# A gated cross-attention block with a routed feed-forward on one Trainium2 core: nine whole expert tiles are moved ahead of the ranking of the last batches

## The reference

```python
x = x + tanh(g_xattn[0]) * xattn(layernorm(x), ctx, mask)      # softmax(x ctx^T / sqrt(512)) ctx
x = x + tanh(g_ffn[0]) * ffn(layernorm(x), w_router, w_gate, w_up, w_down)
# ffn: probs = softmax(xt @ w_router.T); top_v, top_i = top_k(probs, 2); top_v /= sum(top_v)
#      g, u = xt @ w_gate, xt @ w_up (192 wide per expert); act = silu(g) * u
#      out = sum over the two experts of comb * (act @ w_down)
```

## Time and profile before

| what | value |
|---|---|
| three runs | 295.83, 294.32, 295.79 us, median 295.79 |
| the profiled execution | 297.36 us, of it the span from first to last instruction 295.5 us |
| busy: PE, VectorE, ACT, POOL | 88%, 58%, 50%, 55% of the span |
| granted TensorE clock, mean | 0.929 |
| moved by DMA | 52.08 MB, mean 176 GB/s |

### The profile page before, as it was taken

The page is one execution under the profiler, slowest core; times in us unless marked ns, Lnnn a source line. Parts: engine busy times, 40 slices in busy tenths (PEclk is TensorE's granted clock), DMA queues, the critical chain, the costliest instruction groups (busy, mean ns, idle before and its releaser), DMA issues.

```text
span 295.5 us, 5447 instructions
## 1 busy us (share of the span) xinstructions
PE 259.2 (88%) x1501; PEld 220.4 (75%) x1501; DVE 172.2 (58%) x650; ACT 147.3 (50%) x310; POOL 163.9 (55%) x151
## 2 busy tenths in 40 slices
PE   0899998995999978546999999999999999999940
PEld 0777775683867747436899999999999999999930
DVE  4577779996786888992244444344444444444420
ACT  3469856773568544221155555444455444544430
POOL 1256656453455446515236787784884848747461
PEclk9999999999699997556799999999999999999995
DMA  6996888776899634503436588576795886958583
GB/s 207 379 380 197 293 289 293 262 272 222 261 304 328 213 109 152 171 3 87 132 56 114 118 141 148 83 146 133 129 164 100 169 159 104 175 95 159 119 131 50
DMA packets 25950, 52.08 MB, mean 176 GB/s; under 512 B 5248, under 2 KB 5376, under 8 KB 25920
## 3 DMA queue, kind: packets, MB, share of 16 engines
q0 software_dynamic: 8304, 19.83, 36.9%
q1 hardware_dynamic: 17616, 31.89, 32.2%
HBM read 33.81 MB, written 17.89 MB: 175 GB/s over the span
## 4 chain that ended last, share of the span: by engine, by line
PE 63%; DVE 13%; DMA 11%; issue 4%; ACT 3%; SPq 3%; POOL 1%; POOLq 0%; ACTq 0%; DVEq 0%
PE S L1068 9%; PE S L1072 9%; PE S L1069 9%; PE A L1058 6%; DMA out<-X 5%; PE S L930 5%; PE PO L941 4%; DMA x2s<-Y 2%; DVE TB L716 2%; DMA X<-in_x 2%; DVE st L604 2%; PE PL L1091 2%; PE PO L1091 1%; PE PO L1093 1%; PE PL L1095 1%
## 5 line engine op out<-in xcount | busy, mean ns | idle before, releaser
L441 POOL DMA_INDIRECT out<-YT,IXI x36 | 56.8, 1577 | 41.9 <-issue 19.7
L1068 PE MATMUL S<-WGh,XTh 128*128 x144 | 51.8, 360 | 1.0 <-ACT XTh L536 1.0
L1069 PE MATMUL S<-WGl,XTh 128*128 x144 | 48.9, 340 | 0.0
L415 POOL DMA_INDIRECT XG<-x2s,IXG x39 | 38.5, 987 | 18.0 <-issue 9.7
L870 DVE TENSOR_TENSOR H<-SG,S 128x192 f32<-128x192 f32 x36 | 12.7, 354 | 47.8 <-ACT SG L543 41.5
L385 POOL TENSOR_TENSOR WGl<-WGl,WGh 128x512 fp32r<-128x512 f32 x24 | 30.7, 1283 | 16.3 <-ACT WGh L500 16.3
L543 ACT ACTIVATE SG<-S 128x192 f32<-128x192 f32 x36 | 11.9, 330 | 50.1 <-PE S L1072 46.0
L376 POOL TENSOR_TENSOR rs<-mv,CS 128x1 f32<-128x1 f32 x32 | 17.7, 554 | 32.6 <-DVE mv L610 32.6
L863 DVE TENSOR_TENSOR XTl<-A,XTh 128x512 fp32r<-128x512 f32 x37 | 25.6, 691 | 13.6 <-ACT XTh L536 13.1
L941 PE MATMUL PO<-CX,PT 128*128 128x512 f32 x64 | 31.2, 609 | 1.3 <-DVE X L650 1.3
L930 PE MATMUL S<-CT,XLT 128*128 128x256 f32 x128 | 31.7, 392 | 0.0
(11 more groups left out here) (153 smaller groups left out, 548.0 us busy)
## 6 DMA issues: line engine op xcount, KB each, us to landing
WGl<-in_wgu SPq DMA_DIRECT2D x24, 256.0 KB, 4.6
X<-in_x SPq DMA_DIRECT2D x16, 256.0 KB, 4.0
CT<-in_ctxt SPq DMA_DIRECT2D x8, 512.0 KB, 5.8
CX<-in_ctxn SPq DMA_DIRECT2D x8, 512.0 KB, 5.5
out<-X SPq DMA_DIRECT2D x16, 256.0 KB, 4.7
x2s<-Y SPq DMA_DIRECT2D x16, 256.0 KB, 4.8
WD1l<-in_wd SPq DMA_DIRECT2D x8, 256.0 KB, 4.5
WS<-in_wd SPq DMA_DIRECT2D x8, 256.0 KB, 4.5
```

Of the source, the lines that this page charges most:

```text
L415: pool.indirect_dma_start(out=XG[:, j % NX, :], out_offset=None, in_=x2s, in_offset=bass.IndirectOffsetOnAxis(ap=IXG[:, j:j + 1], axis=0))\
L441: pool.indirect_dma_start(out=out, out_offset=bass.IndirectOffsetOnAxis(ap=IXI[:, j:j + 1], axis=0), in_=YT[:, j % NB, :], in_offset=None, ...
L1068: pe.matmul(o, XTh[:, j % 2, c, :], WGh[:, bass.ds(e, 1), c, :], start=(c == 0), stop=False)
L1069: pe.matmul(o, XTh[:, j % 2, c, :], WGl[:, bass.ds(e, 1), c, :], start=False, stop=False)
```

## The change

Nine tiles (`NE`) of the first `EB` = 4 batches are listed, gathered and run while the last batches are still ranked. A tile is whole when its expert has a further 128 rows after four batches. By the counts above twelve are whole (2, 1, 1, 1, 2, 2, 2, 1); the first nine are of the experts 0, 0, 1, 2, 3, 4, 4, 5, 5. The other 27 live tiles follow, again from expert 0: 2, 3, 4, 4, 3, 3, 4, 4 tiles. At tile 9 POOL waits for all earlier adds whatever the expert.

All 40 weight units are split in attention, up to three in a step, and the tile loop holds none. The expert buffers (XG, XTh, XTl, SG, H, HTh, HTl, YT) lie over those of attention (X, CT, CX, XL, XLT, P, PT) so that each gather waits only for the stores of the X tiles under its buffer; ranking's own buffers are outside that overlay. Since ranking goes on during the first tiles, the tile loop uses one bank for transposes (A0), one for the down product (PO), and the bank of gate and up (S0, S1) also for the activation's transposes. On PE, VectorE, ACT and POOL the ends of attention and ranking stand between the parts of tiles 0 to 8, by an order written out by hand (`SIDES` gives VectorE's side steps after mul, coef and hlo of each tile). Two of the exponentials for the router's weights are made on POOL (`odds`), so that ACT keeps the table for Silu.

```diff
-SPLIT = [0, 1, 1] + [2] * 15 + [1] * 4
-NUA = NU - 4
-HOLD = [3, 5, 7, 9]
+SPLIT = [0, 1, 1, 3, 2, 3, 3, 2, 3, 3, 2, 3, 3, 3, 2, 3, 3]
+EB = 4
+NE = 4 * EB - 7
+NEP = (NE + 3) // 4 * 4
+NL = 32
+SIDES = [(2, 2, 5), (2, 2, 3), (1, 1, 2), (1, 1, 2), (2, 2, 2), (2, 2, 3), (1, 3, 4), (2, 1, 2)] + [(0, 0, 0)] * 31
...
             def loadw(u):
+                if u >= NST:
+                    sp.wait_ge(s_wh, u - NST + 1)
...
+            def odds(b):
+                pool.wait_ge(s_dd, b + 1)
+                pool.wait_ge(s_cb, b)
+                pool.tensor_tensor(out=e2[:, :, 0], in0=euler.to_broadcast([128, 2]), in1=dd[:, :, 0], op=ALU.pow)\
+                    .then_inc(s_e2, 1)
+            def stored(*tiles):
+                pool.wait_ge(s_y2, max(tiles) + 1)
+                for k in tiles:
+                    pool.wait_ge(s_so[k % NXT], 16 * (k // NXT + 1))
...
+            for s in range(NTK + 3):
+                for u in units(s - 1)[0:1]:
+                    lo(u)
+                if 0 <= s - 3 < NTK:
+                    rstd(mv2, s - 3, rs2, s_st2, s_rs2)
+                if s == NTK + 2:
+                    odds(6)
+                    stored(13)
+                    gather(3)
+                for u in units(s - 1)[1:]:
+                    lo(u)
+                if s + 2 < NTK:
+                    rstd(mv1, s + 2, rs1, s_st1, s_rs1)
+                if s == NTK:
+                    pool.wait_ge(s_ixe, 1)
+                    pool.wait_ge(s_sy[0], 16 * EB)
+                    pool.wait_ge(s_sy[1], 16 * EB)
+                    pool.wait_ge(s_scb[0], 16 * EB)
+                    stored(9, 10)
+                    gather(0)
+                    stored(11)
+                    gather(1)
+                if s == NTK + 1:
+                    stored(12)
+                    gather(2)
...
+            stored(14, 15)
+            for j in range(4, NX):
                 gather(j)
...
             for j in range(NT):
                 with lives(pool, live, j):
+                    if j == 1:
+                        odds(7)
                     pool.wait_ge(s_y, j + 1)
-                    if j:
+                    if j == NE:
+                        landed(j)
+                    elif j:
                         fence(j)
...
+                    if j + NX == NE:
+                        pool.wait_ge(s_ixg, 1)
+                        pool.wait_ge(s_sy[0], 16 * 8)
+                        pool.wait_ge(s_sy[1], 16 * 8)
+                        pool.wait_ge(s_scb[1], 16 * (B - EB))
                     if j + NX < NT:
                         gather(j + NX)
-                    if j in HOLD:
-                        lo(NUA + HOLD.index(j))
...
+            side += [coefs(5), top2(6), taken()]
+            weave(queue(x2(14), first_xlo(), nbias(mv2, rs2, nb2, 14, s_rs2, s_nb2), x2(15)), 2)
+            side += [slots(5), ranks(6), coefs(6),
+                     braid(slots(6), queue(top2(7), braid(ranks(7), coefs(7)))),
+                     braid(slots(7), left()), last_tiles()]
             live = None
             for j in range(NT):
                 with lives(dve, live, j):
                     mul(j)
+                    if j == 0:
+                        for _ in nbias(mv2, rs2, nb2, 15, s_rs2, s_nb2):
+                            pass
...
+                    steps(SIDES[j][0])
                     if j + 1 < NT:
                         xlo(j + 1)
...
                     coef(j)
+                    steps(SIDES[j][1])
                     hlo(j)
+                    steps(SIDES[j][2])
...
+            tp(14)
+            score(15)
+            first_list()
+            pv(14)
+            rt(12)
+            t2(13)
+            tp(15)
...
+            pe.wait_ge(s_ixe, 1)
...
             tx(0)
+            pv(15)
+            rt(13)
+            own, live = experts(0, ERE, 0), None
+            pe.wait_ge(s_wl, NU)
             for j in range(NT):
                 with lives(pe, live, j):
                     gu(j, own[j])
+                    if j == 0:
+                        t2(14)
+                    if j == 1:
+                        t2(15)
+                        rt(14)
                     if j + 1 < NT:
                         tx(j + 1)
+                    if j == 0:
+                        cum(5)
+                    if j == 2:
+                        tab(5)
+                        cum(6)
+                    if j == 4:
+                        cum(7)
+                        count()
+                    if j == 5:
+                        tab(6)
+                    if j == 6:
+                        last_list()
+                        tab(7)
...
                     if j >= 1:
                         down(j - 1, own[j - 1])
+                    if j == 1:
+                        rt(15)
+                    if j == 6:
+                        last_rows()
                     th(j)
+                    if j == 0:
+                        tab(4)
```

More of the change, by code:

```diff
@@ L266, in units @@
         def units(s):
-            return range(*[min(NUA, sum(SPLIT[:max(0, n)])) for n in (s, s + 1)])
+            return range(*[min(NU, sum(SPLIT[:max(0, n)])) for n in (s, s + 1)])
         STEPS = NTK + 9
@@ L333, in _ @@
                     loadw(u)
-                if s == NTK + 3:
-                    for u in range(NUA, NU):
-                        loadw(u)
                 k = s - 4
@@ L414, in gather @@
                     pool.wait_ge(s_cj, j - NX + 1)
-                pool.indirect_dma_start(out=XG[:, j % NX, :], out_offset=None, in_=x2s,
-                                        in_offset=bass.IndirectOffsetOnAxis(ap=IXG[:, j:j + 1], axis=0))\
+                rows, at = (x2s[0:EB * S, :], IXE[:, j:j + 1]) if j < NE else (x2s, IXG[:, j - NE:j - NE + 1])
+                pool.indirect_dma_start(out=XG[:, xg(j), :], out_offset=None, in_=rows,
+                                        in_offset=bass.IndirectOffsetOnAxis(ap=at, axis=0))\
                     .then_inc(s_g[j % NX], 16)
@@ L428, in fence @@
                     landed(j)
-            for j in range(NX):
+            rstd(mv1, 0, rs1, s_st1, s_rs1)
+            rstd(mv1, 1, rs1, s_st1, s_rs1)
+            for s in range(NTK + 3):
[23 more added lines that the diff above has]
+                    gather(2)
@@ L556, in yev @@
                     act.wait_ge(s_add[j % NB], 16 * (j // NB))
-                act.activation(YT[:, j % NB, :], (PO, PL)[j % 2][:, :], ACT.Copy, scale=cj[:, j % 4:j % 4 + 1])\
+                act.activation(YT[:, j % NB, :], PO[:, :], ACT.Copy, scale=cj[:, j % 4:j % 4 + 1])\
                     .then_inc(s_y, 1)
+            xln(0)
+            for s in range(NTK + 1):
+                if 0 <= s - 4 < NTK:
+                    ev2(s - 4)
+                if s < NTK:
+                    ev1(s)
+                if s + 1 < NTK:
+                    xln(s + 1)
+                if 0 <= s - 2 < NTK:
+                    evp(s - 2)
+                if s >= 7 and s % 2 == 1 and (s - 7) // 2 < B:
+                    weigh((s - 7) // 2)
+                if 0 <= s - 3 < NTK:
+                    x2ln(s - 3)
+                if 0 <= s - 1 < NTK:
+                    exp(s - 1)
+                for u in units(s):
+                    hi(u)
+            ev2(13)
+            evp(15)
+            weigh(5)
+            act.activation(rsum[:, 0:1], rinv[:, 0:1], ACT.Silu)
             xhi(0)
+            x2ln(14)
             live = None
@@ L658, in top2 @@
                 for i in range(2):
[L659 removed]
+                    n = mark(dve.max(out=mx[:, i, :], in_=PL[:, 8 * i:8 * i + 8]))
                     yield
```

567 lines of the change are left out of this document (323 added, 244 removed).

## The result

| | before | after |
|---|---|---|
| median of four runs each | 295.39 us (294.32 to 295.83) | 301.47 us (299.39 to 303.34) |
| ratio, 95% interval | | 1.019 (1.0129 to 1.025) |
| the profiled execution | 297.36 us, span 295.5 | 300.6 us, span 298.8 |
| busy: PE, VectorE, ACT, POOL | 88%, 58%, 50%, 55% | 86%, 59%, 49%, 55% |

A forecast was written before the change was run, and what follows sets the result against it. POOL's queue of scatters and fences was to set the end: IXG at 155.9 (102.3 + 4 + 13.6 + 23.5 + 4.5 + 1.9 + 6.1) plus 136.9 gives 292.8, 2.7 below 295.5; forecast 293.1 us, range 286 to 301.

The forecast's parts named there:

- The price of a fence step: POOL's tile queue: a step with a fence takes 6.3 us from scatter to scatter, a plain one 3.17.
- Rival 1: Tile loop: PE, not POOL, sets the end if a fence step costs under 5.3 us; 283.7 us, chance 0.15.
- Attention, +4: Up to score(15), 102.32 before: loading 40 weight units instead of 32 adds 4 us, ends -5 and +12.
- cost nothing of their own: Attention: eight more ACT copies and POOL subtractions (8 x 1.28) add no time, the engines being busy 36.6 and 28.9 of 56.3 us.
- From score(15) to the first tile, 13.6: After attention: PE waits for the 40th unit, done 13.6 us after score(15)'s start; first tile at 119.9 instead of 140.2.
- Tiles 0 to 5, 29.9: First six tiles: 23.5 us for tiles, 4.5 for PE work moved into them, 1.9 for a VectorE stall.
- the list 6.1 us into tile 6: Tile 6: the last index list, IXG, is ready 6.1 us after the tile's start, at 155.9.
- Rival 2: Attention: it stretches by +12 instead of +4, the index list comes later than 160 us, end 301; chance 0.22.
- POOL waits for IXG before gather(9): POOL's queue after scatter(3): POOL waits for the list IXG, near 155.9, with scatters 4, 5 and 6 queued behind.
- scatter(3) is through by about 153: POOL's early queue: scatter(1) from near 138.4, 2 and 3 behind fences of 6.3 each, scatter(3) done near 153.
- the one at 4 has long landed: POOL's queue after IXG: the fence before scatter(4) costs nothing, leaving ten fences to pay, 63.0 us.
- The queue from scatter(4) on: POOL after IXG and gather(9): ten fence steps 63.0 us, nineteen plain 60.2, the last two 4.4.

The follow-up runs named there:

- e6: Changed kernel, each tile's rows added into a DRAM tensor of its own, sum over experts left out, and no fences; 287.68 us, ratio 0.9706.
- e7: Kernel before with six further unconditional waits for all earlier adds, thirteen in all, nothing else; 309.53 us, ratio 1.0446.
- e3: Changed kernel, where the expert changes POOL issues gather(j+6) before the fence instead of after scatter(j); 290.12 us, ratio 0.9822.
- e8: Kernel before with only the new weight split, all 40 units in attention and none in the tile loop; 300.24 us, ratio 1.012.
- e11: Kernel before plus eight 256 KB DRAM-to-DRAM copies on SP's queue in attention, no added engine work; 300.78 us, ratio 1.02.
- e9: e8 with POOL's subtraction cut to 64 of 512 columns in gate, up and upper down units; 293.17 us, ratio 0.9955.
- e2: Changed kernel with another order of the weight units of experts 5 and 7 and SP's wait count adapted; 299.13 us, ratio 1.0108.
- e4: Changed kernel with the edits of e1, e2 and e3 together; 285.74 us, ratio 0.9636.
- e13: e8 with both reciprocal roots ahead of the second and third subtraction in each of POOL's steps; 298.82 us, ratio 1.0079.
- e10: Kernel before, its own 32-unit split, POOL's subtraction cut to 64 of 512 columns in gate, up and upper down units; 289.22 us, ratio 0.9863.
- e14: Changed kernel with POOL's subtraction cut to 64 of 512 columns in gate, up and upper down units; 297.33 us, ratio 1.0035.
- e1: Changed kernel with odds(7), the exponential of batch 7 on POOL, moved one tile later; 299.33 us, ratio 1.0099.

## Why the prediction was wrong

It had 293.1 us and -2.7; the time is 301.47, just outside the range of 286 to 301 and with the other sign. On the span the sum gave 292.8 and the trace has 298.8. The other 2.4 us of the 8.4 are the scale: the sum put the median 0.3 us above the span of before, while the median after lies 2.7 above its own.

**The bound was named rightly.** POOL's queue sets the end, by e6, e7 and e3. The price of a fence step, the term that the text called decisive, was 6.3. (Its 6.1 from the rows took off a subtraction that lies inside a fence's wait; the six steps of the kernel before, read one by one, average 6.3.) Between scatters 4 and 35 are 126.5 us where the sum had 127.6. With nineteen plain steps at 3.18 and two last ones at 1.9 the ten fences come out at 6.2 each. The 4.2 us estimated from the rule of the Trainium skill (DMA: Bandwidth & Descriptors, section Anatomy of one DMA) is not borne out for these indirect adds: 6.2 here. Rival 1 falls with it. One bank instead of two for transposes and the down product cost nothing that shows: with PE as the bound, in e6, the 21 steps from scatter(12) to scatter(33) take 3.92 us each, the period of the earlier trace rows.

**The terms that failed**, in order, with the time by which each moved the end:

1. *Attention, +4* was +7.4 (score(15) at 109.75), 3.4 more. It is the load of the weights: e8 has +7.8 from that part alone. The base of the term, 102.32, is one trace of an attention that ends at 99.31 in another; the stall of 66 to 77, which the prediction let vanish or come again, differs from trace to trace of the same code. The parts seen, each from its own run and not to be added: bytes and issues 2.1 to 5.1 us (e11, by copies that go another way), the short subtraction 3.7 (e9), the late buffer WS about 2 (e2, e4), the roots behind the second and third subtraction 1.4 at most (e13). The rest of the split is open. The reason given for "cost nothing of their own", a busy share of 28.9 of 56.3 us, is no reason: in the ranking of the kernel before the subtractions take 4.8 us (e10), with 40 units in attention 3.7 (e9). What the eight further ones cost by themselves no run separates.
2. *From score(15) to the first tile, 13.6* was 15.0, 1.4 more. The path was the one forecast, x2(14), rstd(14), two subtractions. x2(14) with its statistics ends at 121.02, 11.3 us after score(15) and not 10.3, and the 40th unit is done at 124.11. PE was not ready then: tx(0) had waited 2.66 us for the gather, pv(15) ran for 3.75 us where pv(14) took 1.96, and rt(13) behind it took 1.72 where 0.8 was forecast, which is the other 0.7. e14 gives 4.0 of this stretch back, at the full clock.
3. *Tiles 0 to 5, 29.9* were 29.0, and *the list 6.1 us into tile 6* was there after 4.95. So IXG came at 158.75, 2.9 us after the forecast, where the first tile was 4.9 late. Rival 2 put its bound at 160; it explains half of the miss.
4. *"POOL waits for IXG before gather(9)", "scatter(3) is through by about 153" and "the one at 4 has long landed".* Beside the size of point 1, this is the step that failed. `odds(7)` stands ahead of scatter(1) and waits for a side step of tile 3; the prediction listed POOL's scatters and gathers and left this instruction out. Scatter(3) came at 157.80, there was no wait for IXG, and scatter(4) paid its whole fence: 4.94 us from IXG to scatter(4), not 1.3. That is 3.6 us, by itself more than the forecast's gain. e1 gives the structure of the forecast back: scatter(3) at 153.26 and the wait for IXG.
5. *The queue from scatter(4) on* took 1.1 us less, *the tail* 8.6 us instead of 8.0.

Points 1 to 3 make the 2.9 of IXG. Together +2.9 + 3.6 - 1.1 + 0.6 = +6.0, the 298.8. Even with point 4 mended the change is not faster (e1, 1.0099): the gain of 2.7 was smaller than the 3.4 by which the attention term was off, inside its ends of -5 and +12, and 0.53 for faster was too much for a result that hung on it.

**What the gain of 13.5 us turned into:** six further expert changes on the queue that had no room left. The prediction saw that; it did not ask whether the 3 us idle in each fence could hold the gather, which turns the slower kernel into a faster one.

## What to carry to other kernels

When work is split in an early and a late group, count what is paid per change of group (here 7 expert changes became 13, at 3 us of pure waiting each), on the queue that pays for it. In a queue that waits for landings, put every issue that doesn't depend on the landing ahead of the wait. List *all* instructions of the bounding queue, the small ones with foreign waits above all, and don't cost POOL's elementwise work at nothing because its busy share is low: look at the longest duration of tiny VectorE instructions beside it, over all of them. And before a shift of a few us in one trace is given a cause, look at what the same code does in another.

## What the runs showed of the hardware

- A VectorE instruction of 128x16 elements takes 0.16 us at its shortest and 1.22 beside a POOL subtraction of 1.27. Another order on POOL moves the hold to other instructions: between e8 and e13 the four of MS fell from 5.0 to 0.6 us and those of cc rose from 0.6 to 3.8.
- pv(15) ran at 3.75 us, pv(14) at 1.96. Ahead of pv(15) PE had been idle for 2.66 and 0.66 us; the granted clock from 119.68 to 123.43 is 0.50, the lower of the two levels, 1.2 GHz. In e14 PE had been idle for 2.40 us, and pv(15) ran at 1.88 with a granted clock of 1.00.
- A second gather issued between an add and the wait for its landing does not lengthen the wait for the landing: the nine fence steps from scatter(7) on average 6.22 us in e3, with two gathers, and 6.22 in the change, with one.
- The same attention code ended at 99.31, 101.79 and 102.32 us in three traces.
